# Fetching attention's first pair during the projection, and reordering stores and loads around that border

## The chip, the cores and the metric

The kernel runs on one core of a Trainium2 chip. Its time is the device time of one execution, in microseconds; of several runs the median is given.

## The reference, cut to what matters

Four blocks follow one another on x (4 batches of 1024 tokens, 256 wide), each with a residual: a state-space layer, a mixture of 8 experts, causal attention with 16 heads of 16, and a mixture of 16 experts. The change lies in the third.

```python
x = x + _L0_attn_ref(_layernorm(x, axis=-1), ...)      # state-space layer
x = x + _L0_ffn_ref(_layernorm(x, axis=-1), ...)       # mixture of experts
x = x + _L1_attn_ref(_layernorm(x, axis=-1), L1_attn_W_qkv, L1_attn_W_o)
x = x + _L1_ffn_ref(_layernorm(x, axis=-1), ...)       # mixture of experts

# _L1_attn_ref
qkv = jnp.einsum('bsi,oi->bso', x, W_qkv)
Q, K, V = jnp.split(qkv, 3, axis=-1)
Q, K, V = (to_heads(Q), to_heads(K), to_heads(V))
Q, K = (apply_rope(Q), apply_rope(K))
scores = jnp.einsum('bhqd,bhkd->bhqk', Q, K) / jnp.sqrt(jnp.float32(d_k))
scores = jnp.where(causal, scores, -jnp.inf)
attn = jax.nn.softmax(scores, axis=-1)
out = jnp.einsum('bhqk,bhkd->bhqd', attn, V)
```

## The kernel before, in words

The program is a row of phases, each an `nc.Block()` in which the five engines run their own instruction lists in order and meet at its end. Two of them matter here, with a short block between that clears semaphores (L2413).

`project_qkv` (L1231) works through the 4096 tokens in 8 groups of 512. A tick handles several groups at once, each at another step:

- GpSimd gathers the two expert outputs of each token (L1339, 8 gathers a group, half of them ahead of `rsqrt` and half behind), and later adds the turned halves (`add_turned`, L1353 and L1355).
- DVE adds the experts to x (L1383, L1387), takes the statistics, multiplies by the rotation's tables (`rotate`, L1416), adds the last sum (L1407) and makes the low part of queries and keys (`rest`, L1421): qk minus its rounded high part.
- ScalarE normalises (L1453), copies the values out of PSUM (`copy_v`, L1467), copies the transposed tokens (L1460) and rounds queries and keys to the high part (`round_qk`, L1476).
- TensorE transposes and projects (L1503, L1514, L1521).
- SP (the sync engine) issues all direct DMAs, in this order in tick t: `store_x2(t)` (L1295), `load(t+2)` of x (L1291), `store_v(t-1)` (L1299, 512 KB), `store_qk(t-3)` (L1311 for the high, L1313 for the low parts, 8 DMAs of 256 KB, each with a wait for ScalarE's or DVE's part). At the end it waits for all stores. `round_qk(g)` waits for the stores of group g-2, whose buffers it fills.

ScalarE's order in tick t is `normalise(t)`, `copy_v(t-1)`, `copy_xn(t)`, `round_qk(t-2)`; the ticks run to 9. TensorE has nothing after group 7's values in tick 7.

`attention` (L1537) works through 32 pairs of heads (8 per batch). Queries and keys of a pair lie in one of four buffers (`qs`, `ks`); 8 DMAs of 128 KB bring them (`load(p)`, L1656, issue at L1649), each 32 rows of 4 KB to 16 partitions. All of them land in partitions 0 to 63; row 96 of `qs` gets the negated row maxima. TensorE's list is written out by step, 18 steps a pair. In a step it does, for pair q, one chunk of scores with keys in the rows (`chunk`, L1841), and for a pair one and a half ahead one or two pieces of scores with queries in the rows (`piece`, L1827), whose maxima DVE takes (L1766). After a pair's pieces the maxima are transposed (L1833), negated by ScalarE (L1778) and written by SP into the pair's buffer (`row`, L1671); `chunk(p, 0)` waits for that row. ScalarE takes the exponentials (L1785), GpSimd masks them (L1738) after it has laid out the values (L1730), and TensorE multiplies them with the values (L1857). Until pair 0 has its row, TensorE fills the steps with matmuls that compute nothing (`keep_busy`, L1864), 7 of them ahead of the first piece. `piece(p, 0)` waits for the pair's 8 loads.

SP's order is: `load(0)` (4 DMAs of queries; the 4 of keys are issued by ScalarE at L1795), `load(1)`, then in tick 1 `row(0)`, `load(2)`, `load_v(0)` (L1664, 1 MB of values); in tick t from 2 on `load(t+1)`, now and then `load_v`, `store(t-4)`, `row(t-1)`. `load(p)` for p of 4 or more waits for the last chunk of pair p-4. At step 72 ScalarE issues a fetch of expert weights (4 MB in two DMAs, L2491).

Of the kernel before, what the change touches and what calls it, by code (L numbers as in the profile page):

```python
# [4 lines left out]
FP32 = mybir.dt.float32  # L5
# [1224 lines left out]

def project_qkv(nc, sb, pb, sem, c, x_dram, outputs, kept, sum_dram, w_qkv_dram, rope_dram, qkt_dram, v_dram):  # L1231

# [50 lines left out]
    def live(g):  # L1283
        return 0 <= g < groups

    with nc.Block() as block:
        @block.sync
        def _(sp):
# [30 lines left out]
            for tick in range(groups + 3):  # L1319
                if live(tick):  # L1320
                    store_x2(tick)
                if live(tick + 2):
                    load(tick + 2)
                if live(tick - 1):
                    store_v(tick - 1)
                if live(tick - 3):
                    store_qk(tick - 3)
            for s in range(2):
# [111 lines left out]
        def _(act):  # L1440
# [36 lines left out]

            for tick in range(groups + 2):
                if live(tick):
                    normalise(tick)  # L1480
                if live(tick - 1):
                    copy_v(tick - 1)
                if live(tick):
                    copy_xn(tick)
                if live(tick - 2):
                    for n in range(NB):
                        round_qk(tick - 2, n)

        @block.tensor
# [46 lines left out]

def attention(nc, sb, pb, sem, c, qkt_dram, v_dram, heads_dram, inv_dram, fetch):  # L1537

# [13 lines left out]
    RT, RS = 3, 4  # L1552
    ks = sb("t_ks", [P, 2 * RINGQ, SEQ], FP32R)
    qs = sb("t_qs", [P, 2 * RINGQ, SEQ], FP32R)
    v_raw = sb("t_v_raw", [P, NC, DM])
# [62 lines left out]
    filled, set_up = sem("t_filled"), sem("t_set_up")  # L1618
    qk_loaded = [sem(f"t_qk_loaded{s}") for s in range(RINGQ)]
    row_loaded = [sem(f"t_row_loaded{s}") for s in range(RINGQ)]  # L1620
# [22 lines left out]
    def live(p):  # L1643
        return 0 <= p < pairs

    def load_rows(eng, p, dst, which, part, hl):
        s = p % RINGQ
        rows = hl * 2 * DM + which * DM + (p % PAIRS) * 2 * HD
        eng.dma_start(dst[part * HD:(part + 1) * HD, 2 * s:2 * s + 2, :].bitcast(FP32),  # L1649
                      qkt_dram[rows:rows + 2 * HD, bass.ts(p // PAIRS, SEQ)].rearrange("(h d) t -> d h t", h=2)).then_inc(qk_loaded[s], 16)  # L1650

    with nc.Block() as block:
        @block.sync
        def _(sp):
            def load(p):
                wait(sp, st_done, NX * (p - RINGQ) + NX)  # L1656
                for part in range(4):
                    load_rows(sp, p, qs, 0, part, part % 2)
                    if p > 0:
                        load_rows(sp, p, ks, 1, part, part // 2)  # L1660

# [4 lines left out]
            def row(p):  # L1666
                s = p % RINGQ
                if p < RINGQ:
                    sp.wait_ge(rows_filled, 2 * p + 1)
                sp.wait_ge(neg_ready, p + 1)  # L1670
                sp.dma_start(qs[MAX_ROW:MAX_ROW + 1, 2 * s:2 * s + 2, :].bitcast(FP32).rearrange("o h (c q) -> o (h c) q", c=NC),  # L1671
                             neg_max[:, p % 2, :].bitcast(FP32)).then_inc(row_loaded[s], 16)
# [4 lines left out]

            load(0)
            load(1)
            for tick in range(1, pairs + 5):  # L1680
                if tick > 1 and live(tick + 1):
                    load(tick + 1)
                if tick % PAIRS == PAIRS // 2 and live(tick + PAIRS // 2):
                    load_v(tick // PAIRS + 1)
                if live(tick - 4):
                    store(tick - 4)
                if live(tick - 1):
                    row(tick - 1)
                if tick == 1:
                    load(2)  # L1690
                    load_v(0)
                if tick == pairs:
                    for s in range(2):
                        sp.wait_ge(stored[s], 8 * PAIRS * (BATCH - 1))
                    sp.wait_ge(vs_ready, BATCH)
                    for b in range(BATCH - 1):
                        sp.dma_start(sums[:, b, :], sums_of_batch(heads_dram, b)).then_inc(sums_loaded, 16)
                if tick == pairs + 1:
                    sp.wait_ge(inv_ready, 1)
                    for b in range(BATCH - 1):  # L1700
                        sp.dma_start(inverse_of_batch(inv_dram, b), sums[:, b, :]).then_inc(inv_stored, 16)
# [5 lines left out]
        def _(pool):  # L1707
            def zero_rows(p):
                nc.gpsimd.memset(qs[KS:P, 2 * p:2 * p + 2].bitcast(FP32), 0.0).then_inc(rows_filled, 1)

# [8 lines left out]
            for p in range(1, RINGQ):  # L1719
                zero_rows(p)  # L1720
                nc.gpsimd.memset(ks[KS:P, 2 * p:2 * p + 2].bitcast(FP32), 1.0).then_inc(rows_filled, 1)
            pool.wait_ge(rows_filled, 2 * RINGQ - 1)
# [27 lines left out]
        def _(dve):  # L1750
            nc.vector.memset(row_max[:], 0.0).then_inc(filled, 1)
            nc.vector.memset(ks[KS:P, 0:2].bitcast(FP32), 1.0).then_inc(filled, 1)
            nc.vector.memset(ps_o[:], 0.0).then_inc(filled, 1)
# [19 lines left out]
        def _(act):  # L1773
# [19 lines left out]

            for part in range(4):
                load_rows(act, 0, ks, 1, part, part // 2)  # L1795
            for step in range(LAST):
# [12 lines left out]
        def _(pe):  # L1809
# [9 lines left out]
            def piece(p, x):  # L1819
                head, qc, k0, keys = row_pieces[p % 2][x]  # L1820
                at = 2 * (p % RINGQ) + head
                if x == 0:
                    pe.wait_ge(qk_loaded[p % RINGQ], 128 * (p // RINGQ + 1))
                    if p < RINGQ:
                        pe.wait_ge(rows_filled, 2 * p + 1)
                bank_free(p, x)
                nc.tensor.matmul(bank_of(p, x)[:, 0:keys], qs[0:MAX_ROW, at, qc * P:(qc + 1) * P], ks[0:MAX_ROW, at, k0:k0 + keys],  # L1827
                                 start=True, stop=True).then_inc(s_done, 1)
# [6 lines left out]
            def chunk(p, i):  # L1835
                at = 2 * (p % RINGQ) + i // NST
                if i == 0:
                    pe.wait_ge(row_loaded[p % RINGQ], 16 * (p // RINGQ + 1))
                wait(pe, exp_ready, NX * p + i - RT + 1)
                for kc, q0, col, width in chunks[i % NST]:  # L1840
                    last = nc.tensor.matmul(ps_st[(NX * p + i) % RT][:, col:col + width], ks[:, at, kc * P:(kc + 1) * P], qs[:, at, q0:q0 + width],  # L1841
                                            start=True, stop=True)
# [509 lines left out]
def build(nc, x, w_in, w_abc, w_out, norm_w, gate_w, gate_b, w1, b1, w2, b2, w_qkv, w_o, rope, w_route, w_gu, w_d,  # L2352
# [36 lines left out]
    with ExitStack() as whole:  # L2389
        keep = lambda n, s, d=FP32: whole.enter_context(nc.sbuf_tensor(n, s, d))  # L2390
        sem = lambda n: whole.enter_context(nc.semaphore(n))
        moe0_loaded, moe1_loaded = sem("moe0_loaded"), sem("moe1_loaded")

        x_in = flat(x)
        with ExitStack() as first:
# [13 lines left out]


            phase(project_qkv, c, x1_dram, outputs[0], kept, x2_dram, w_qkv, rope, qkt_dram, v_dram)

# [6 lines left out]
        wgu_sb = wsb("wgu_sb", [P, KD, E1 * 2 * F1])  # L2419
        phase(attention, c, qkt_dram, v_dram, headst_dram, inv_dram, lambda eng: load_moe1_up(eng, moe1_loaded, wgu_sb, w_gu))  # L2420
        wd_sb = wsb("wd_sb", [P, F1 // P, E1 * DM])
# [116 lines left out]
```

## Time and profile before

| | us |
|---|---|
| median of 3 runs | 1808.42 |
| lowest, highest | 1807.4, 1811.73 |
| the profiled execution | 1807.72 |
| its span, from the first to the last instruction | 1805.7 |

The profile is of one execution. Times in its rows count from the start of the span. PE is TensorE's matmuls, PEld its weight loads, DVE VectorE, ACT ScalarE, POOL GpSimd, SP the sync engine; a q behind a name is the engine's instruction queue, which issues DMAs. PEclk is the granted clock of TensorE: 1.00 is 2.4 GHz and 0.50 is 1.2 GHz. The projection lies at 750 to 914 us, attention at 915 to about 1427.

### The profile page before, as it was taken

To read this page: it belongs to the slowest core of one execution; us is meant where nothing else is said; L and a number is where in the kernel's file an instruction comes from. 1 tells how busy PE (TensorE), PEld (TensorE's weight loads), DVE (VectorE), ACT (ScalarE), POOL (GpSimd) and SP (SyncE) were. 2 spreads that over 40 slices of the span, in tenths; PEclk is the share of its full clock that TensorE was granted. 3 is DMA by queue.
4 is the path that set the end of the run, shared out by engine and by line. 5 is a ranking of instruction groups with operands and counts; after the bars stand their busy time and mean duration, and the time that the engine had idled before them with its cause. 6 is when DMAs were issued, how large, how long until landed. Compare 5 with 4: busy or idle time off the path is not lost. (4 is left out here: it accounts for less than half of the span.)

```text
span 1805.7 us, 29737 instructions
## 1 busy us (share of the span) xinstructions
PE 1558.0 (86%) x9335; PEld 1100.6 (61%) x9335; DVE 1000.2 (55%) x3322; ACT 721.5 (40%) x1519; POOL 563.2 (31%) x991
## 2 busy tenths in 40 slices
PE   1999999982999999688668899999999667399998
PEld 0577777771666666444345566666666356288787
DVE  1245444442222222268847788888888267365566
ACT  0444444430222222134305676777777422144410
POOL 2122333344000000278532322333222238500076
PEclk9899999995999999898878999999999877599999
DMA  8100111112222221359767867667664276445444
GB/s 297 55 24 25 47 48 48 36 52 93 73 65 65 65 65 59 102 177 298 230 134 107 190 94 116 90 93 116 94 90 66 74 224 223 168 147 158 135 138 142
DMA packets 150807, 204.08 MB, mean 113 GB/s; under 512 B 20352, under 2 KB 119168, under 8 KB 150400
## 3 DMA queue, kind: packets, MB, share of 16 engines
q1 hardware_dynamic: 102496, 129.53, 32.0%
q10 hardware_dynamic: 35872, 39.09, 6.4%
q0 software_dynamic: 12288, 33.57, 5.9%
q8 instruction: 80, 1.31, 0.3%
q14 instruction: 71, 0.58, 0.1%
HBM read 116.91 MB, written 84.93 MB: 112 GB/s over the span
## 5 line engine op out<-in xcount | busy, mean ns | idle before, releaser
L1785 ACT ACTIVATE t_probs<-t_ps_st 128x512 f32<-128x512 f32 x576 | 313.4, 596 | 145.0 <-PE t_ps_st L1841 135.3
L1766 DVE CUSTOM_DVE_ANT_0 t_seen<-t_ps_s,t_later 128x512 bf16<-128x512 f32 (+3 forms) x512 | 286.1, 587 | 34.9 <-PE t_ps_s L1827 32.5
L1827 PE MATMUL t_ps_s<-t_ks,t_qs 96*128 96x512 f32 (+3 forms) x768 | 252.6, 369 | 5.9 <-DMA t_ks<-qkt_dram 5.7
L1841 PE MATMUL t_ps_st<-t_qs,t_ks 128*128 128x512 f32 (+3 forms) x768 | 245.8, 369 | 12.0 <-DMA t_qs<-t_neg_max 6.4
L1738 POOL TENSOR_SCALAR_AFFINE_SELECT t_probs<-t_probs 128x128 f32<-128x128 f32 x512 | 137.3, 302 | 319.3 <-ACT t_probs L1785 317.5
L1841 PEld LDWEIGHTS t_ps_st<-t_qs,t_ks 128*128 128x128 f32 x768 | 138.8, 192 | 87.2 <-ACT t_probs L1785 42.3
L1766 DVE CUSTOM_DVE_ANT_0 t_seen<-t_ps_s,t_later,t_first_max 128x512 bf16<-128x512 f32 (+3 forms) x256 | 140.6, 549 | 54.8 <-PE t_ps_s L1827 54.8
L1339 POOL DMA_INDIRECT d_ye<-outputs_dram,r_pos_all x64 | 64.6, 1009 | 327.5 <-POOLq L1099 309.7
L1857 PE MATMUL t_ps_o<-t_probs,t_vs 128*17 128x256 f32 (+1 forms) x2560 | 156.6, 364 | 0.5 <-issue 0.5
L1827 PEld LDWEIGHTS t_ps_s<-t_ks,t_qs 96*128 96x128 f32 x768 | 141.9, 194 | 24.3 <-DMA t_ks<-qkt_dram 6.5
L832 PE MATMUL ps_h<-w_in,xnt 128*128 128x512 f32 x256 | 125.5, 615 | 22.4 <-ACT xnt L666 22.4
L1131 PE MATMUL m_ps_h<-w_sb,m_xt 128*128 x284 | 135.6, 600 | 0.0
L1146 PE MATMUL m_ps_y<-w_sb,m_ht 128*128 x568 | 134.2, 379 | 0.0
L1202 ACT ACTIVATE m_xt<-m_ps_x 128x256 f32<-128x256 f32 x150 | 57.6, 384 | 174.8 <-PE m_ps_x L1124 174.6
L1174 DVE TENSOR_TENSOR m_h<-m_ps_h,b_sb 128x512 f32<-128x512 f32 x71 | 49.1, 692 | 131.6 <-PE m_ps_h L1131 129.7
L2268 POOL DMA_INDIRECT f_ye<-outputs_dram,r_pos_all x64 | 63.1, 986 | 170.8 <-POOLq L1099 151.6
L1212 ACT ACTIVATE m_ht<-m_ps_ht 128x128 f32<-128x128 f32 (+1 forms) x150 | 63.9, 426 | 128.0 <-PE m_ps_ht L1139 128.0
L1146 PEld LDWEIGHTS m_ps_y<-w_sb,m_ht 128*128 128x128 f32 x568 | 102.5, 190 | 11.0
L1857 PEld LDWEIGHTS t_ps_o<-t_probs,t_vs 128*17 128x17 f32 x2560 | 59.3, 97 | 72.9 <-issue 28.8
L1124 PE MATMUL m_ps_x<-ident,m_x_t 128*128 128x128 f32 x300 | 58.9, 279 | 41.4 <-DMA m_x_t<-gathered_dram 40.3
L351 POOL TENSOR_TENSOR xi<-xi,sig_z 128x512 f32<-128x512 f32 x32 | 40.6, 1269 | 160.3 <-ACT sig_z L678 160.2
L1185 DVE TENSOR_TENSOR m_y<-m_ps_y,b_sb 128x256 f32<-128x256 f32 x71 | 30.2, 425 | 104.7 <-PE m_ps_y L1146 104.7
(309 smaller groups left out, 2782.0 us busy)
## 6 DMA issues: line engine op xcount, KB each, us to landing
m_x_t<-gathered_dram SPq DMA_DIRECT2D x150, 128.0 KB, 2.0
outputs_dram<-m_y ACTq DMA_DIRECT2D x150, 128.0 KB, 1.7
t_qs<-qkt_dram SPq DMA_DIRECT2D x128, 128.0 KB, 5.8
t_ks<-qkt_dram SPq DMA_DIRECT2D x124, 128.0 KB, 6.1
qkt_dram<-d_hi SPq DMA_DIRECT2D x32, 256.0 KB, 4.0
qkt_dram<-d_lo SPq DMA_DIRECT2D x32, 256.0 KB, 4.0
headst_dram<-t_att SPq DMA_DIRECT2D x32, 256.0 KB, 7.1
x_t<-in_x_dram SPq DMA_DIRECT2D x8, 512.0 KB, 4.4
```

The costliest lines, as they stand in the source:

```text
L832: last = nc.tensor.matmul(ps_h[h][:], xnt[:, n % 2, j, :], w_in[:, j, h * DI:(h + 1) * DI], start=(j == 0), stop=(j == KD - 1))
L1131: last = nc.tensor.matmul(ps_h[t % 2][:], xt[:, t % 2, j, :], w_up[:, j, bass.ts(expert[t], width)], start=(j == 0), stop=(j == KD - 1))
L1146: last = nc.tensor.matmul(ps_y[t % 2][:], ht[:, t % 2, j, :], w_down[:, j, bass.ts(expert[t], DM)], start=(j == 0), stop=(j == blocks - 1))
L1212: nc.scalar.activation(ht[:, t % 2], ps_ht[t % 2][:], ACT.Relu if relu else ACT.Copy).then_inc(ht_ready, 1)
L1339: nc.gpsimd.indirect_dma_start(out=ye[:, g % 2, j, i, :], out_offset=None, in_=outputs[:, :], in_offset=bass.IndirectOffsetOnAxis(ap=kept[ ...
L1738: nc.gpsimd.affine_select(out=diag, in_=diag, compare_op=ALU.is_ge, fill=0.0, base=0, pattern=[[1, P]], channel_multiplier=-1).then_inc(ma ...
L1766: nc.vector.tensor_tensor_reduce(out=seen[:, (NP * p + x) % (RS + 1), 0:keys], in0=bank_of(p, x)[:, 0:keys], in1=masks, scale=1.0, scalar= ...
L1785: nc.scalar.activation(probs[:, p % 2, i // NST, base:base + STC], ps_st[(NX * p + i) % RT][:], ACT.Exp, scale=HD ** -0.5).then_inc(exp_re ...
L1827: nc.tensor.matmul(bank_of(p, x)[:, 0:keys], qs[0:MAX_ROW, at, qc * P:(qc + 1) * P], ks[0:MAX_ROW, at, k0:k0 + keys], start=True, stop=Tru ...
L1841: last = nc.tensor.matmul(ps_st[(NX * p + i) % RT][:, col:col + width], ks[:, at, kc * P:(kc + 1) * P], qs[:, at, q0:q0 + width], start=Tr ...
L1857: last = nc.tensor.matmul(ps_o[32 * g:32 * g + VR, col:col + width], vs[:, (p // PAIRS) % 2, kc, 2 * (p % PAIRS) + head, :], probs[:, p % ...
L2268: nc.gpsimd.indirect_dma_start(out=ye[:, g % R, j, i, :], out_offset=None, in_=outputs[:, :], in_offset=bass.IndirectOffsetOnAxis(ap=kept[ ...
```

## The change

- `project_qkv` gets a function `fetch`. ScalarE calls it at tick 8, after two waits for the stores of groups 0 and 1: it issues the 8 loads of pair 0.
- Pair 0's buffers (`q_first`, `k_first`) and semaphore are therefore made before the projection and handed to both phases; `qs` and `ks` become lists of four buffers each. ScalarE's four loads at the start of attention and SP's `load(0)` go.
- In the projection SP issues `store_qk(t-3)` ahead of `store_v(t-1)`.
- In tick 8 ScalarE does `copy_v(7)` after `round_qk(6)` instead of before it.
- In attention SP issues `load(2)` in tick 1 ahead of `row(0)`; behind `row(0)` comes `load_v(0)` alone, and then `load(3)`.

```diff
-def project_qkv(nc, sb, pb, sem, c, x_dram, outputs, kept, sum_dram, w_qkv_dram, rope_dram, qkt_dram, v_dram):
+def project_qkv(nc, sb, pb, sem, c, x_dram, outputs, kept, sum_dram, w_qkv_dram, rope_dram, qkt_dram, v_dram, fetch):
...
                     load(tick + 2)
+                if live(tick - 3):
+                    store_qk(tick - 3)
                 if live(tick - 1):
                     store_v(tick - 1)
-                if live(tick - 3):
-                    store_qk(tick - 3)
...
             for tick in range(groups + 2):
+                if tick == groups:
+                    for s in range(2):
+                        act.wait_ge(qk_stored[s], 32 * NB)
+                    fetch(act)
                 if live(tick):
                     normalise(tick)
-                if live(tick - 1):
+                if live(tick) and live(tick - 1):
                     copy_v(tick - 1)
                 if live(tick):
                     copy_xn(tick)
                 if live(tick - 2):
                     for n in range(NB):
                         round_qk(tick - 2, n)
+                if tick == groups:
+                    copy_v(tick - 1)
...
+def load_head_rows(eng, p, dst, which, part, hl, qkt_dram, loaded):
+    rows = hl * 2 * DM + which * DM + (p % PAIRS) * 2 * HD
+    eng.dma_start(dst[part * HD:(part + 1) * HD].bitcast(FP32),
+                  qkt_dram[rows:rows + 2 * HD, bass.ts(p // PAIRS, SEQ)].rearrange("(h d) t -> d h t", h=2)).then_inc(loaded, 16)
+
+
+def load_heads(eng, p, q, k, qkt_dram, loaded):
+    for part in range(4):
+        load_head_rows(eng, p, q, 0, part, part % 2, qkt_dram, loaded)
+        load_head_rows(eng, p, k, 1, part, part // 2, qkt_dram, loaded)
...
-    ks = sb("t_ks", [P, 2 * RINGQ, SEQ], FP32R)
-    qs = sb("t_qs", [P, 2 * RINGQ, SEQ], FP32R)
+    ks = [k_first] + [sb(f"t_ks{i}", [P, 2, SEQ], FP32R) for i in range(1, RINGQ)]
+    qs = [q_first] + [sb(f"t_qs{i}", [P, 2, SEQ], FP32R) for i in range(1, RINGQ)]
...
-    qk_loaded = [sem(f"t_qk_loaded{s}") for s in range(RINGQ)]
+    qk_loaded = [first_loaded] + [sem(f"t_qk_loaded{s}") for s in range(1, RINGQ)]
...
             def load(p):
                 wait(sp, st_done, NX * (p - RINGQ) + NX)
-                for part in range(4):
-                    load_rows(sp, p, qs, 0, part, part % 2)
-                    if p > 0:
-                        load_rows(sp, p, ks, 1, part, part // 2)
+                load_heads(sp, p, qs[p % RINGQ], ks[p % RINGQ], qkt_dram, qk_loaded[p % RINGQ])
...
-            load(0)
             load(1)
             for tick in range(1, pairs + 5):
-                if tick > 1 and live(tick + 1):
+                if live(tick + 1):
                     load(tick + 1)
...
                 if tick == 1:
-                    load(2)
                     load_v(0)
...
-            for part in range(4):
-                load_rows(act, 0, ks, 1, part, part // 2)
...
+            q_first, k_first = (ahead.enter_context(nc.sbuf_tensor(n, [P, 2, SEQ], FP32R, side="right")) for n in ("t_qs0", "t_ks0"))
+            phase(project_qkv, c, x1_dram, outputs[0], kept, x2_dram, w_qkv, rope, qkt_dram, v_dram,
+                  lambda eng: load_heads(eng, 0, q_first, k_first, qkt_dram, first_loaded))
```

The rest of the diff hands the buffers through and puts `qs[s]` for `qs[:, 2 * s:...]`.

## Rows read from the trace of the kernel before

**Rows 1.** The page, busy time of each engine with its share of the span.

```profile
PE 1558.0 (86%) x9335; PEld 1100.6 (61%) x9335; DVE 1000.2 (55%) x3322; ACT 721.5 (40%) x1519; POOL 563.2 (31%) x991
```

**Rows 2.** The timeline 860 to 935: start, duration, engine, line, what, [idle before].

```profile
891.43 0.36 SPq L1299 DMA_DIRECT2D v_dram<-d_v  x1
...
902.08 2.50 DVE L1421 TENSOR_TENSOR d_lo<-d_qk,d_hi 128x512 f32<-128x512 f32 x4 [4.89 <-ACT d_hi L1476]
...
909.99 0.70 SPq L1313 DMA_DIRECT2D qkt_dram<-d_lo  x1
```

**Rows 3.** Windows: length, busy (instructions) of each engine, PEclk, DMA share, GB/s.

```profile
870.00:878.00 8.00, 3.77 (x17) 2.57 (x16) 7.97 (x17) 2.33 (x5) 6.25 (x4) 0.98 0.33 111
878.90:912.90 34.00, 11.67 (x34) 6.35 (x32) 19.57 (x26) 8.39 (x16) 9.79 (x6) 0.70 0.85 277
...
895.00:910.00 15.00, 0.00 (x0) 0.00 (x0) 4.58 (x6) 2.19 (x4) 3.31 (x2) 0.50 1.01 332
```

**Rows 4.** The timeline 914 to 969: attention's first issues and TensorE's waits for DMAs.

```profile
914.97 1.79 ACTq L1649 DMA_DIRECT2D t_ks<-qkt_dram  x4
...
915.01 7.63 PE L1864 MATMUL t_ps_st<-causal,ident 128*128 128x512 f32 x14 [24.23 <-PEq L2413]
...
926.45 0.79 PE L1827 MATMUL t_ps_s<-t_ks,t_qs 96*128 96x512 f32 x1 [3.82 <-DMA t_ks<-qkt_dram]
...
927.41 0.69 DVE L1766 CUSTOM_DVE_ANT_0 t_seen<-t_ps_s,t_later 128x512 bf16<-128x512 f32 x1 [9.44 <-PE t_ps_s L1827]
...
955.21 0.50 PE L1827 MATMUL t_ps_s<-t_ks,t_qs 96*128 96x512 f32 x1 [1.88 <-DMA t_ks<-qkt_dram]
...
968.02 0.80 PE L1841 MATMUL t_ps_st<-t_qs,t_ks 128*128 128x512 f32 x1 [4.83 <-DMA t_qs<-t_neg_max]
```

**Rows 5.** Windows of attention's start: PE, PEld, DVE, ACT, POOL, PEclk, DMA share, GB/s.

```profile
920.00:925.00 5.00, 2.64 (x8) 1.04 (x6) 0.00 (x0) 0.00 (x0) 5.00 (x4) 1.00 1.07 127
926.40:932.20 5.80, 5.75 (x15) 4.74 (x16) 2.80 (x10) 0.00 (x0) 5.74 (x3) 0.50 1.01 120
927.40:935.00 7.60, 7.60 (x28) 6.35 (x26) 5.37 (x19) 0.00 (x0) 4.83 (x2) 0.68 0.67 79
935.00:942.00 7.00, 7.00 (x36) 6.14 (x35) 6.94 (x29) 0.00 (x0) 0.00 (x0) 1.00 0.00 0
956.00:973.00 17.00, 11.98 (x45) 8.00 (x44) 7.96 (x29) 6.20 (x12) 7.09 (x25) 0.61 1.08 144
```

**Rows 6.** The timeline of SP's queue: the rows of maxima of pairs 0, 1, 2, 4, 5.

```profile
943.47 0.59 SPq L1671 DMA_DIRECT2D t_qs<-t_neg_max  x1
...
958.70 0.54 SPq L1671 DMA_DIRECT2D t_qs<-t_neg_max  x1
...
981.36 0.51 SPq L1671 DMA_DIRECT2D t_qs<-t_neg_max  x1
...
1017.55 0.52 SPq L1671 DMA_DIRECT2D t_qs<-t_neg_max  x1
...
1032.05 0.52 SPq L1671 DMA_DIRECT2D t_qs<-t_neg_max  x1
```

**Rows 7.** The timeline at 865, DVE's first addition of group 7.

```profile
865.67 1.98 DVE L1383 SCALAR_TENSOR_TENSOR d_part<-d_ye,r_prob_all,d_x 128x256 f32<-128x256 f32 x4 [1.81 <-issue]
```

**Rows 8.** The timeline 880 to 892: low parts of group 5, group 7's values, group 6's low parts.

```profile
880.94 3.56 DVE L1421 TENSOR_TENSOR d_lo<-d_qk,d_hi 128x512 f32<-128x512 f32 x4
...
889.08 0.60 ACT L1467 ACTIVATE d_v<-d_ps_v 128x512 f32<-128x512 f32 x1 [7.25 <-PE d_ps_v L1521]
...
891.96 3.56 DVE L1421 TENSOR_TENSOR d_lo<-d_qk,d_hi 128x512 f32<-128x512 f32 x4 [1.00 <-ACT d_hi L1476]
```

**Rows 9.** The timeline at 944, the first of pair 2's loads on SP's queue.

```profile
944.11 0.58 SPq L1649 DMA_DIRECT2D t_qs<-qkt_dram  x1
```

**Rows 10.** The rows of maxima (L1671), all 32, from issue to landing.

```profile
DMA to landing us min/median/max: 1.8/1.8/9.3
```

**Rows 11.** The timeline at 992, ScalarE's second issue of expert weights.

```profile
992.03 6.77 ACTq L2491 DMA_DIRECT2D wgu_sb<-in_w_gu_dram  x1
```

## What the change should do to the time, worked out before its run

> **What bounds the kernel now.** I read first the page's totals: TensorE is busy for 86% of the span [rows 1], and only where it stands still, or runs slowly, is there much to be had. The change touches the end of the projection and the start of attention, so every cost is read from that stretch, 860 to 1032 us. The views are the order of time of SP's queue, windows with the DMA share and the granted clock, and the rows in which TensorE sat idle for a DMA.
>
> The projection ends on transfers. DVE's last low part is done by 904.6 and still the next block starts only at 914.97, because SP issues 24 stores of 256 KB back to back behind v_dram's store at 891.43, the last at 909.99 [rows 2, 4]. From 895 to 910 the DMA engines are full: share 1.01 at 332 GB/s. From 870 to 878 the share is 0.33 [rows 3]. So the bound there is the DMA engines' work, and SP's 0.79 us per issue follows it.
>
> Attention starts on transfers too. TensorE waits 3.82 us for pair 0, 1.88 us for pair 2 and 4.83 us for pair 1's row of maxima [rows 4]. After each wait its clock falls to the lower level: granted 0.50 in 926.4 to 932.2 and 0.61 in all of 956 to 973, against 1.00 at 935 to 942 [rows 5]. What this costs is read in the spacing of the rows of maxima, one per pair: 15.23 and 22.66 us at the start, 36.19 for the next two together, and 14.50 from there on [rows 6].
>
> **The change, part by part.** (1) The projection's stores. SP issues store_qk(t-3) ahead of store_v(t-1). In ticks 3 to 6 the same bytes flow, some us earlier in each tick. A tick's 2.1 MB of stores (6.3 us at 332 GB/s) then lie behind x2's store and x's load, and are still there when the tick's last gather is issued, so the gather meets other traffic as before. DVE's whole wait ahead of add_experts is 1.81 us in such a tick [rows 7]. I take 0 and keep -1 and +3.6 (half of that wait in four ticks) as bounds.
>
> At the end it counts. Group 4's stores move from 879 on to 870 to 877, where the DMA engines have room. Group 5's move from 891.8 to 880.3 and on: their low parts come from 881.6 to 884.5 [rows 8]. Behind v's store at 891.4 there are 16 stores instead of 24. If SP's issue were the bound, the end would come 8 x 0.79 = 6.3 us earlier.
>
> (2) The fetch of pair 0 by ScalarE: eight loads of 128 KB at its tick 8. The waits ahead of them are for groups 0 and 1, stored long before. ScalarE stood idle there for 7.25 us, up to 889.08, until TensorE had the last values [rows 8]. At 0.45 us each (four took 1.79 [rows 4]) the issues end near 885.5. Queued behind them are round_qk(6) and then copy_v(7). The rounding fits into what is left of the gap, and copy_v(7) can't start before 889.08, so no value is delayed; DVE, which waited 1.00 us for that rounding [rows 8], no longer does. The fetch isn't free on the DMA engines, though: such loads move at 127 GB/s with the share at 1.07 [rows 5]. 1.05 MB is 8.3 us of full DMA.
>
> Sum by DMA work: from 878.9 (v's store) to 912.9 it is 0.85 x 34 = 28.9 us [rows 3]. Group 4 leaves (6.3) and the fetch comes (8.3): 30.9. No gap is left but about 1 us around 880.5, as the low parts arrive one by one. The end is 878.9 + 30.9 + 1 = 910.8 instead of 912.9, some **2.0 us** saved. The bounds are 6.3 (issue alone) and -1 (the tail takes the fetch whole against group 5's stores, 8.3 against 6.3, and gives back 1 us by the earlier low parts).
>
> One rule of the Trainium skill prices the fetch otherwise. DMA: Bandwidth & Descriptors, Specifications, has pieces of 512 B or more run at line rate and gives about 358 GB/s for HBM to one core. By that the fetch, in rows of 4 KB, would be an estimated 2.9 us, and the saving would be the 6.3 of the issues. This case's row, 127 GB/s at share 1.07 [rows 5], disagrees, and the measurement decides.
>
> (3) Attention's start. Pair 0 is there, so after its 14 warming matmuls (915.01 to 922.64) TensorE goes straight on: **3.8 us**. DVE's fills and the mask were done by 918, since DVE stood idle for 9.44 us ahead of its first piece [rows 4]. TensorE stays at the higher clock too. In 927.4 to 935 DVE is busy for 5.37 of 7.6 us, and for 6.94 of 7 once the clock is up [rows 5]. So DVE is the next bound and **2.2 us** go; by the clock alone it would be 2.9 (5.8 us at half). Nothing at all, if another gap cools TensorE, is the lower end.
>
> (4) Pair 2's loads now follow pair 1's at once. Both together are 17 us of DMA, so pair 2 lands some 19 us after the block's start; before, it was wanted 38.4 us in (953.33) [rows 4], and by the new count some 32. Pair 1 lands 10 us in and is wanted 21 us in. The 1.88 us go, but DVE had a backlog and its own work per pair stays, so of the 15.23 I count **1.4 us**, with 0.7 (what leaves 14.5) and 1.9 as bounds.
>
> (5) Behind row(0) SP now has only the values and pair 3. Before, pair 2 lay ahead of them (from 944.11 [rows 9]), so row(1), issued at 958.70 on the same queue, landed 9.3 us later, where the median is 1.8 [rows 6, 10]. Now values (1.05 MB at the stores' rate, 3.2 us) and pair 3 (8.3 to 9 us) end 13 to 14 us behind row(0); row(1) is issued 13.8 to 14.5 behind it and lands by 17, and chunk(1,0) wants it 4.5 us after its issue (963.19 against 958.70), so about 18.5. The wait of 4.83 goes, and with it the lower clock of 956 to 973. The interval 22.66 becomes 14.5: **8.2 us**. The lower end is 4.8, the wait alone.
>
> What is late next: ScalarE's own fetch of expert weights, whose second issue holds it for 6.77 us [rows 11]. It is tied to step 72 and stays, and so do the 36.19 us. All behind attention moves as one block.
>
> Sum: 2.0 + 3.8 + 2.2 + 1.4 + 8.2 = 17.6 us. The profiled execution took 1807.72 us (span 1805.7), 0.7 under the median of 1808.42. 1807.72 - 17.6 = 1790.1, and by the median **1790.8 us**.
>
> **The rivals.** A: the waits go, but TensorE stays at the lower clock in part of the start. Then 2.0 + 3.8 + 0 + 0.7 + 4.8 = 11.3 us go: 1797. For it speaks the 0.61 over 17 us after a wait of only 1.88 [rows 4, 5]; against it, that the clock is 1.00 from 935 to 942 with the same work. Chance 0.13.
>
> B: row(1) is still caught behind pair 3, since its margin is some 1.5 us and the time of a pair's loads is known to 10%. If it lands 3 us late the clock falls again: 2.0 + 3.8 + 2.2 + 1.4 + 2 = 11.4, again 1797. Chance 0.12.
>
> C: the stores are bound by issue, and the gathers gain: 6.3 + 3.6 in place of 2.0, in sum 25.5: 1783. Against it speaks share 1.01 [rows 3]. Chance 0.12.
>
> D, slower: ScalarE is held by its own DMA issues. Place: tick 8, ahead of round_qk(6) and copy_v(7). If each of the eight took 6.77 us, as the second weight fetch does [rows 11], ScalarE would be free at 936 instead of 885.5. v's store and 16 stores (14.2 us of DMA) would follow, so the stage would end some 39 us later, less the 15.6 us of attention: 1832. It decides for slower once the eight together take over 24 us, 3 us each. Against it: the four issues at 914.97 beside SP's took 1.79 us in all [rows 4]. Chance 0.03.
>
> E: the fetch takes DMA time from the tail, and attention only swaps the later waits for others of DVE and ScalarE: -1 + 3.8 in sum, 1805.6. Chance 0.04.
>
> **How the numbers follow.** Forecast (12 to 22 us saved): 0.56. With A, B and most of C, the range 1783 to 1799 holds about 8 in 10. About 0.3%, 5.4 us, is what a measurement can tell from no change here. Faster by more: 0.56 + 0.13 + 0.12 + 0.12, of which I keep 0.92. Within 0.3%: 0.05. Slower: 0.03.
>
> **What would show it.** In the changed kernel's profile the block behind the projection starts about 2 us earlier, with the DMA share near 1 from 881 to the end. TensorE's first piece follows the warming matmuls without a gap, at a granted clock of 1.00. The first row of maxima is issued 22.5 us after the block's start instead of 28.5, and the next ones 13.8 and 14.5 apart. No wait of TensorE for pair 2 or for row(1) is left. It would be wrong if the clock falls anyway, if row(1) still lands over 5 us after its issue, or if ScalarE's eight issues take over 8 us.

## The result

| | us |
|---|---|
| before, median | 1808.42 |
| after, median of 5 runs | 1789.04 (1786.89 to 1790.61) |
| after over before | 0.9888, 95% interval 0.9875 to 0.9901 |
| the profiled execution of after, and its span | 1787.32, 1785.6 |

The forecast was 1790.8, 17.6 us less; 19.4 came. The changed kernel run again beside other kernels gave 1788.47 against 1809.03, ratio 0.9888. In the two traces 20.1 us of the span are gone, and by the sixth row of maxima 20.4 (1011.65 instead of 1032.05), so what lies behind that row took back only 0.3.

SP's queue in the changed kernel, from x2's last store to the rows of maxima of pairs 0 to 2 and 5. The first load at 912.60 is attention's start:

```profile
872.11 0.36 SPq L1295 DMA_DIRECT2D x_dram<-d_x  x1
...
894.84 0.37 SPq L1299 DMA_DIRECT2D v_dram<-d_v  x1
...
907.38 0.69 SPq L1313 DMA_DIRECT2D qkt_dram<-d_lo  x1
912.60 0.34 SPq L1545 DMA_DIRECT2D t_qs<-qkt_dram  x1
...
933.97 0.59 SPq L1680 DMA_DIRECT2D t_qs<-t_neg_max  x1
...
947.34 0.54 SPq L1680 DMA_DIRECT2D t_qs<-t_neg_max  x1
960.87 0.51 SPq L1680 DMA_DIRECT2D t_qs<-t_neg_max  x1
...
1011.65 0.51 SPq L1680 DMA_DIRECT2D t_qs<-t_neg_max  x1
```

Set against [rows 2, 4, 6], the stretches are these (x2(3) and x2(7) are the stores of x2 in ticks 3 and 7, at 808.26 and 869.26 before, 808.36 and 872.11 after):

| stretch | before | after | measured | forecast |
|---|---|---|---|---|
| x2(3) to x2(7), four ticks | 61.00 | 63.75 | +2.75 | 0 |
| x2(7) to attention's start | 45.71 | 40.49 | -5.22 | -2.0 |
| attention's start to row(0) | 28.50 | 21.37 | -7.13 | -6.0 |
| row(0) to row(1) | 15.23 | 13.37 | -1.86 | -1.4 |
| row(1) to row(2) | 22.66 | 13.53 | -9.13 | -8.2 |
| row(2) to row(5) | 50.69 | 50.78 | +0.1 | 0 |

Attention's start looks as forecast. The timeline of TensorE shows the 14 warming matmuls, and the first piece right behind them with no wait in brackets, where [rows 4] had 3.82:

```profile
912.64 7.39 PE L1869 MATMUL t_ps_st<-causal,ident 128*128 128x512 f32 x14 [18.45 <-PEq L2420]
...
919.68 0.58 PE L1832 MATMUL t_ps_s<-t_ks,t_qs 96*128 96x512 f32 x1
```

And the windows of the changed kernel (PE, PEld, DVE, ACT, POOL, PEclk, DMA share, GB/s): a full clock (1.00) and DVE busy all the time in 925 to 932. The first row is the end of the projection, to be held against the 0.85 and 277 of [rows 3]:

```profile
881.50:910.30 28.80, 11.99 (x32) 6.59 (x32) 20.72 (x26) 9.12 (x17) 9.80 (x6) 0.74 0.97 294
...
925.00:932.00 7.00, 7.00 (x37) 6.15 (x35) 7.00 (x29) 0.00 (x0) 4.87 (x2) 1.00 0.80 90
```

### The profile page after: what moved, and what is told of

It is laid out like the page before. It is cut to its first block and busy times, and to the rows that moved or that the text cites. A ratio compares the mean times of both kernels' runs of the same rounds, so it can differ in the third digit from the quotient of the medians.

```text
span 1785.6 us, 29738 instructions
## 1 busy us (share of the span) xinstructions
PE 1557.8 (87%) x9335; PEld 1100.2 (62%) x9335; DVE 999.4 (56%) x3322; ACT 721.7 (40%) x1519; POOL 564.4 (32%) x991
## 5 line engine op out<-in xcount | busy, mean ns | idle before, releaser
L1832 PE MATMUL t_ps_s<-t_ks,t_qs 96*128 96x512 f32 (+3 forms) x768 | 248.7, 364 | 0.5 <-ACT t_neg_max L1785 0.5
L1773 DVE CUSTOM_DVE_ANT_0 t_seen<-t_ps_s,t_later,t_first_max 128x512 bf16<-128x512 f32 (+3 forms) x256 | 140.6, 549 | 50.8 <-PE t_ps_s L1832 50.8
L1832 PEld LDWEIGHTS t_ps_s<-t_ks,t_qs 96*128 96x128 f32 x768 | 139.5, 191 | 18.1 <-DVE t_first_max L1773 1.6
```

Of the source, the lines that this page charges most:

```text
L1773: nc.vector.tensor_tensor_reduce(out=seen[:, (NP * p + x) % (RS + 1), 0:keys], in0=bank_of(p, x)[:, 0:keys], in1=masks, scale=1.0, scalar= ...
L1832: nc.tensor.matmul(bank_of(p, x)[:, 0:keys], q[0:MAX_ROW, head, qc * P:(qc + 1) * P], k[0:MAX_ROW, head, k0:k0 + keys], start=True, stop=T ...
```

## The experiments

The experiments ran on three chips, each beside the kernel before. On the first of them (e1 to e4) all kernels were slower, the kernel before at 1831.72 us, so times are compared by their ratios, and stretches within the projection and attention by the traces. How well unchanged code repeats differs by stretch. The ticks in the old order repeat within 0.3 us (60.69 to 61.00), in the new order only within 3 (62.04 to 65.02). The first row comes 27.15 to 28.50 us after attention's start without the fetch (e5 apart, whose edit moves it) and 21.19 to 22.75 with it. The kernel before and e8 have the same attention, and their next two intervals are 15.23 and 22.66 against 16.25 and 21.36.

The end repeats least: the old code took 45.71 us in the kernel before, 45.48 in e7 and 48.74 in e5. TensorE's clock makes that difference: the projection of group 7's queries and keys (16 matmuls) took 7.11 us in e7, 7.99 in the kernel before and 10.16 in e5, with a granted clock of 1.00, 0.70 and 0.50 over its first 3 us, and v's last store follows it. The timelines of TensorE in e7 and then e5:

```profile
877.46 7.11 PE L1514 MATMUL d_ps_qk<-d_xnt,d_w_qk 128*128 128x512 f32 x16 [0.77 <-DVE d_by L1416]
```

```profile
877.81 10.16 PE L1514 MATMUL d_ps_qk<-d_xnt,d_w_qk 128*128 128x512 f32 x16 [0.77 <-DVE d_by L1416]
```

The end can be taken apart at v's last store. In every kernel but e1 that store is issued 14.2 us plus the time of these 16 matmuls after x2(7) (7.11 to 10.17 us; 8.54 in the changed kernel). From it to attention's start it is 23.54, 24.18 and 24.39 us in the kernel before, e7 and e5, which have 24 stores behind it, 23.91 in e1, and 17.66 to 18.16 in all kernels with 16 stores behind it. This second part repeats within 1 us, and it is the better measure of what an edit does.

In the table "ticks" is x2(3) to x2(7), "end" is x2(7) to attention's start, "rows" are the first row's distance from that start and the next two intervals.

| kernel | ratio (95%) | ticks | end | rows |
|---|---|---|---|---|
| before | 1 | 61.00 | 45.71 | 28.50, 15.23, 22.66 |
| changed | 0.9888 (0.9875 to 0.9901) | 63.75 | 40.49 | 21.37, 13.37, 13.53 |
| changed again (c1) | 0.9888 (0.9867 to 0.9909) | 63.99 | 40.71 | 21.31, 13.38, 13.53 |
| e1 old store order | 0.9927 (0.9904 to 0.9949) | 60.75 | 50.31 | 21.19, 13.38, 13.53 |
| e2 new order from tick 7 | 0.9870 (0.9851 to 0.9889) | 60.73 | 41.93 | 21.68, 13.39, 13.75 |
| e3 no fetch ahead | 0.9920 (0.9891 to 0.9948) | 62.04 | 41.53 | 28.37, 13.39, 13.53 |
| e4 pair 2 behind row(0) | 0.9944 (0.9924 to 0.9964) | 63.89 | 41.94 | 22.11, 15.30, 22.93 |
| e5 before, warm gap | 0.9994 (0.9979 to 1.0008) | 60.69 | 48.74 | 25.70, 15.25, 22.98 |
| e6 values copied first | 0.9890 (0.9847 to 0.9934) | 65.02 | 40.21 | 22.75, 13.38, 13.54 |
| e7 before, pair 2 early | 0.9922 (0.9903 to 0.9941) | 60.75 | 45.48 | 27.15, 13.39, 13.52 |
| e8 before, new order alone | 0.9990 (0.9978 to 1.0002) | 63.99 | 42.02 | 27.49, 16.25, 21.36 |
| e9 new order from tick 6 | 0.9879 (0.9857 to 0.9901) | 61.57 | 41.71 | 21.70, 13.38, 13.53 |
| e10 e9, weights in two steps | 0.9869 (0.9845 to 0.9894) | 61.90 | 41.80 | 21.68, 13.39, 13.52 |

**The store order, undone in the changed kernel (e1).**

```diff
-                if live(tick - 3):
-                    store_qk(tick - 3)
                 if live(tick - 1):
                     store_v(tick - 1)
+                if live(tick - 3):
+                    store_qk(tick - 3)
```

> The changed kernel with one part undone: SP stores values ahead of queries and keys in every tick, as before the change. Theory 1 (read from the two traces): the new order has two effects of opposite sign. In ticks 3 to 6 the stores of queries and keys lie ahead of the gathers in the DMA engines, and the four ticks from x2(3) to x2(7) take 63.75 us instead of 61.0; at the end it saves. So with the old order the four ticks take 61.0 again, the end takes the 45.7 us of before from x2(7) to attention's start, with the fetch in the gap ahead of the last values at no cost, and attention starts at about 915.0: 2.4 us later than in the changed kernel, 1791.4. Theory 0 (the prediction's): the ticks don't change, the fetch is 8.3 us of exclusive DMA time and finds only 5 us of gap: attention starts at 918, 1794.4.

The ticks came back to 60.75, as theory 1 has it. But the end took 50.31 us, longer than in the kernel before and than both theories gave. The cause stands in ScalarE's and SP's rows of e1:

```profile
892.90 2.19 ACT L1476 ACTIVATE d_hi<-d_qk 128x512 fp32r<-128x512 f32 x4 [10.64 <-DMA qkt_dram<-d_lo]
...
895.00 1.06 ACT L1467 ACTIVATE d_v<-d_ps_v 128x512 f32<-128x512 f32 x2
...
896.09 0.37 SPq L1299 DMA_DIRECT2D v_dram<-d_v  x1
```

round_qk(6) waits for group 4's stores, which in the old order are issued together with the fetch and land late. ScalarE stands for 10.64 us, copy_v(7) waits behind it, and v's store goes out 26.4 us after x2(7) instead of 22.2 in the kernel before (869.26 to 891.43), with 24 stores behind it. So the fetch and the reordered last tick need the new store order at the end. The end is 9.8 us longer than in the changed kernel. 6.2 us of that lie behind v's store (23.91 instead of 17.76), about what the order is worth by itself. The store itself comes 18.3 us behind x2(7), the 16 matmuls not counted, instead of 14.2: these 4.1 us are the price of the fetch and the reordered tick under the old order (the matmuls, 8.15 us, gave 0.4 back). Which of the two makes them was not tried. The eight issues of the fetch took 7.8 us here (879.83 to 887.59), close to the 8 us that the prediction named as a sign against it.

**The store order, new only at the end (e2, e9).** e2 has it from tick 7, e9 from tick 6:

```diff
-                if live(tick - 3):
-                    store_qk(tick - 3)
-                if live(tick - 1):
+                if tick < groups - 1 and live(tick - 1):
                     store_v(tick - 1)
+                if live(tick - 3):
+                    store_qk(tick - 3)
+                if tick >= groups - 1 and live(tick - 1):
+                    store_v(tick - 1)
```

> The changed kernel with the new store order only from tick 7 on, the old one in ticks 3 to 6. Theory 1: the four ticks take 61.0 us again and the end keeps its 40.5 us from x2(7) to attention's start, so attention starts 2.8 us earlier than in the changed kernel, near 909.8, and the time is 1786.2. Theory 0: the order in ticks 3 to 6 costs nothing, the time is that of the changed kernel, 1789.0.

> The changed kernel with the new store order only from tick 6 on (e2 had it from tick 7 on), where no load of x lies between x2's store and the stores of queries and keys. Theory 1: only ticks with three things queued ahead of the gathers (x2's store, x's load, the stores of queries and keys) lose by the new order, so the four ticks take 61.0 us, and with group 3's stores out of the way of group 4's the end takes the 40.5 us of the changed kernel instead of e2's 41.9. Attention starts 2.8 us earlier than in the changed kernel: ratio to the kernel before 0.9875. Rival: tick 6 loses 1 us as the others do and the clock in tick 8 decides the rest: as e2, 1.3 us before the changed kernel.

The ticks fell to 60.73 and 61.57, so the cost of the new order in the earlier ticks is real. Tick 6 of e9, which has the new order but no load of x, took 15.26 us, as it did with the old one. In e10, whose projection has the same code, tick 6 took 15.79. The end kept most of its gain but was 1.0 to 1.4 us longer than the changed kernel's, so the 40.5 us that theory 1 gave both times were missed. v's store came 23.8 and 23.7 us after x2(7) instead of 22.7, because the 16 matmuls ahead of it took 9.59 and 9.47 us instead of 8.54; TensorE's clock in e9 was 0.50 to 0.62 from 876 to 882. From v's store on it was 18.2 and 18.1 us, against 17.8. Whether the edit or chance gave the lower clock is open. By their traces both start attention earlier than the changed kernel, by 1.35 us (e2, 911.25) and, beside c1 on one chip, by 0.8 us (e9, 910.41 against 911.22). The ratios (0.9870 and 0.9879 against 0.9888) point the same way, with overlapping intervals.

**The store order alone, in the kernel before (e8).** The edit of e1 the other way round.

> The kernel before with the new store order of the projection alone, without fetch or any change in attention. Theory 1: the four ticks take 62 to 64 us instead of 61.0, x2(7) to attention's start 41.5 instead of 45.7 (as without the fetch in e3), so attention starts 1.6 us earlier and the time is 1.6 us less, ratio 0.999. Theory 0: ticks as before and 8 issues of 0.79 us saved, 6.3 us less, ratio 0.9965.

Ticks 63.99, end 42.02: +3.0 and -3.7 us. From v's store to attention's start it is 17.66 us instead of 23.54, the changed kernel's gain in full and without a fetch; the rest of the difference in the end is the 16 matmuls, 10.17 us here. Ratio 0.9990, as theory 1 gave it: alone, the reorder is worth nothing that these runs can tell.

**Why the ticks lose.** The second half of group 4's gathers (tick 3), the kernel before and then the changed one, each with its time from issue to landing:

```profile
L1339 POOL DMA_INDIRECT d_ye<-outputs_dram,r_pos_all x4: 953/978/1057, 811.7 to 815.6; - x4
DMA to landing us min/median/max: 2.7/3.5/4.2
```

```profile
L1339 POOL DMA_INDIRECT d_ye<-outputs_dram,r_pos_all x4: 952/978/1055, 811.8 to 815.7; - x4
DMA to landing us min/median/max: 5.7/5.9/6.1
```

And DVE's addition that waits for them, before and after:

```profile
819.91 1.91 DVE L1383 SCALAR_TENSOR_TENSOR d_part<-d_ye,r_prob_all,d_x 128x256 f32<-128x256 f32 x4 [1.90 <-issue]
```

```profile
821.54 1.67 DVE L1383 SCALAR_TENSOR_TENSOR d_part<-d_ye,r_prob_all,d_x 128x256 f32<-128x256 f32 x4 [3.41 <-issue]
```

The gathers are issued at the same time and land 2.4 us later at the median. In the old order the last of them is issued before the first of the tick's stores of queries and keys (816.01), in the new one these stores go out from 809.32 on. DVE then waits 1.5 us longer; that it is the gathers it waits for is read from the code, since the rows name no releaser. Tick 3 grew by 1.3 us. In the next two ticks the median rose from 4.4 to 5.2 and from 4.1 to 5.2 us, and they grew by 0.4 and 1.0. That the order costs the ticks is shown (e1, e2, e8); that the gathers are how it does is what the traces suggest, and was not tried by itself. The size is uncertain: with this order e3's ticks took 62.04 us and e6's 65.02.

**No fetch ahead (e3).** Pair 0 is loaded at attention's start, the rest is as changed.

```diff
             for tick in range(groups + 2):
-                if tick == groups:
-                    for s in range(2):
-                        act.wait_ge(qk_stored[s], 32 * NB)
-                    fetch(act)
...
+            for part in range(4):
+                load_head_rows(sp, 0, qs[0], 0, part, part % 2, qkt_dram, first_loaded)
             load(1)
...
+            for part in range(4):
+                load_head_rows(act, 0, ks[0], 1, part, part // 2, qkt_dram, first_loaded)
```

> The changed kernel without the fetch in the projection: pair 0 is loaded at attention's start as before (queries by SP, keys by ScalarE), all other parts kept. Theory 1: the fetch was hidden, since it and the stores ran beside each other (294 GB/s over 28.8 us), and attention starts within 0.7 us of the changed kernel's 912.6. Theory 0: the fetch costs the tail at least 2 us, so attention starts at 910.6 or earlier. Both: TensorE waits 3.8 us for pair 0 again and runs its first pieces at the lower clock, so that the first row of maxima comes 28.5 us after attention's start instead of 21.4. In sum 7.1 us more by theory 1, 1796; 5 us by theory 0, 1794.

The end took 41.53 us without the fetch and 40.49 and 40.71 with it, and from v's store on 18.08 against 17.76 and 17.91: with the new order the fetch costs the projection nothing. From 890 to 893.8 the DMA share of e3 is 0.00; the changed kernel's is 1.03 from 892 to 894.8. So the fetch fills a gap ahead of v's store. Attention started at 911.88, within 0.7 us of 912.60, and the first row came 28.37 us after it. So the fetch ahead is worth 7.0 us, all of it in attention; the times say 5.8 (0.9920 against 0.9888), with wide intervals. Why it is cheap shows in the changed kernel's DMA queues from 881 to 893 (packets, MB, share of 16 engines), the fetch being all of q10:

```profile
q1 hardware_dynamic: 1301, 1.93, 57.7%
q10 hardware_dynamic: 384, 1.05, 38.8%
```

38.8% of 12 us is 4.7 us of the DMA engines for the 1.05 MB, in which q1 stored beside it. In the kernel before, where such loads run only beside each other, from 920 to 925:

```profile
q1 hardware_dynamic: 128, 0.36, 61.0%
q10 hardware_dynamic: 103, 0.27, 45.6%
```

1.07 x 5 us for 0.63 MB, or 8.8 us for 1.05 MB. It isn't the second queue that slows them: in the changed kernel SP's queue alone moved 120 GB/s at share 1.05 with such loads (920 to 930). So the share over 1 was a limit of these loads among themselves, and left room for stores. Why it is so is open.

**Pair 2's place (e4, e7).** e4 takes it back in the changed kernel; e7 makes it alone in the kernel before.

```diff
-                if live(tick + 1):
+                if tick > 1 and live(tick + 1):
                     load(tick + 1)
...
                 if tick == 1:
+                    load(2)
                     load_v(0)
```

> The changed kernel with one part undone: pair 2's loads go behind the first row of maxima again, ahead of the values. The prediction's theory: TensorE waits for pair 2 again, then for row(1), which lands some 9 us after its issue, and loses its clock after each. The intervals of the rows go from 13.37 and 13.53 back to 15.2 and 22.7: 11.0 us more, 1800. Rival: only the waits themselves come back (1.9 + 4.8) and the clock costs nothing beside them: 6.7 us more, 1795.7.

> The kernel before with one part done alone: pair 2's loads right behind pair 1's, and only the values and pair 3 behind the first row of maxima. Theory: the wait for pair 0 stays (first row 28.5 us after attention's start), the waits for pair 2 and for row 1 go with their clock, and the intervals are 13.4 and 13.5 us instead of 15.2 and 22.7: 11 us less, ratio 0.994. Rival (pair 2 in the queue delays pair 0 or pair 1, whose loads run at that time): the first row comes later than 28.5 and part of the 11 us is lost.

e4's rows of maxima (pairs 0, 1, 2), then e7's of pairs 1 and 2:

```profile
941.94 0.59 SPq L1680 DMA_DIRECT2D t_qs<-t_neg_max  x1
957.24 0.54 SPq L1680 DMA_DIRECT2D t_qs<-t_neg_max  x1
980.17 0.51 SPq L1680 DMA_DIRECT2D t_qs<-t_neg_max  x1
```

```profile
953.40 0.54 SPq L1671 DMA_DIRECT2D t_qs<-t_neg_max  x1
966.92 0.51 SPq L1671 DMA_DIRECT2D t_qs<-t_neg_max  x1
```

15.30 and 22.93 in e4, 13.39 and 13.52 in e7: 11.3 us of intervals come back in e4 and 11.0 go in e7, and the pair's place alone makes them. TensorE's waits for DMAs in e4 are 2.0 and 4.8 us together, so the other 4.5 us are what comes with them, the lower clock among it. e7 gives 0.9922, about 14 us (11 to 17 by the interval), the largest single part; by the traces it is 11.4 from attention's start to the sixth row. Pair 2 in the queue took nothing from pair 0, whose wait was 3.2 us.

**The clock by itself (e5).** TensorE's wait for pair 0 is filled with matmuls in the kernel before:

```diff
-            for i in range(6):
+            for i in range(10):
                 keep_busy(i, 4 * P)
```

> The kernel before with four more warming matmuls at attention's start (10 instead of 6 blocks), which fill TensorE's 3.8 us wait for pair 0 and take nothing else away. Theory (the clock is a term of its own): the first pieces start as before, some 11.5 us after attention's start, but at the higher clock, and the first row of maxima comes 2.2 to 2.9 us earlier, at 25.6 to 26.3 us instead of 28.5. Rival (the pieces are bound by DVE or by the arriving pair anyway): 28.5 stays. The later waits for pair 2 and row 1 stay in both, so the time changes by less than 3 us.

The matmuls end when the pair is there, and the clock of 925 to 930 is 1.00 instead of 0.55; the row of maxima is counted from SP's first load:

```profile
916.47 2.20 SPq L1649 DMA_DIRECT2D t_qs<-qkt_dram  x5
...
942.17 0.59 SPq L1671 DMA_DIRECT2D t_qs<-t_neg_max  x1
```

```profile
927.89 0.59 PE L1827 MATMUL t_ps_s<-t_ks,t_qs 96*128 96x512 f32 x1
```

```profile
925.00:930.00 5.00, 5.00 (x20) 3.18 (x18) 1.19 (x5) 0.00 (x0) 5.00 (x3) 1.00 1.09 129
```

The first piece runs 11.4 us after attention's start, as before (11.5), and the row comes at 25.70 instead of 28.50. But the kernel before is not the only measure. From the first piece to the row it takes 17.0 us in the kernel before and in e3, and 15.8 in e7 and e8, which waited 3.2 and 3.4 us instead of 3.8 and 3.7: in the 5.8 us from that piece on the clock was 0.50 in the first two and 0.72 and 0.71 in the others. Without the wait (changed kernel, e4, e5, e6) it takes 14.3. So the clock's share is 1.5 or 2.7 us, by how soon it comes back, with the wait left as it was. The ratio, 0.9994, can't tell so little from nothing; the stretch can.

**ScalarE's last tick (e6).**

```diff
-                if live(tick) and live(tick - 1):
+                if live(tick - 1):
                     copy_v(tick - 1)
...
-                if tick == groups:
-                    copy_v(tick - 1)
```

> The changed kernel with one part undone: in its tick 8 ScalarE copies group 7's values ahead of rounding group 6, as before the change; the fetch stays ahead of both. The prediction's theory: DVE waits about 1 us for the rounding again, but the DMA engines are full by then, so the end moves by less: x2(7) to attention's start 40.5 to 41.2 us. Rival (the chain of rounding, low parts and stores sets the end): all of the 1.0 us or more comes back, 41.5 to 42.5.

DVE waits 1.10 us for the rounding again, and the end takes 40.21 us (17.94 from v's store on): the reorder of the last tick moves nothing that can be seen.

**What is left in attention (e10).**

```diff
                 if step == 4 * NX:
-                    fetch(act)
+                    fetch(act, 0)
+                if step == 5 * NX:
+                    fetch(act, 1)
```

> The kernel of e9 with one thing more: ScalarE issues the second half of the expert weights at step 90 instead of right behind the first at step 72. Theory (the prediction's: the intervals of 19.4 and 16.5 us that are left come from ScalarE's hold of 6.3 us at that second issue): the hold goes, and the two intervals fall to 14.5 to 15.5 each: about 6 us less than e9, ratio 0.9845. Rival: the first issue is held in its place, or the 4 MB themselves slow the loads of the pairs, and the two intervals stay at 33 us or more in sum.

ScalarE's second issue takes 0.40 us instead of e9's 6.54, so the hold is gone. But the intervals from row(2) on are 14.58, 17.67 and 16.41, in sum 48.66 against 50.68 in e9. The first one lost 5.0 us and the next two took 3.0 back, TensorE now waiting 3.2 us in two places for a row of maxima. So 2.0 us went instead of the 6 that were expected, and the sum of the first two intervals, 32.25, is short of the rival's 33 too. What holds those rows was not tried. e10 has the lowest ratio beside the kernel before, 0.9869; that it or e9 or e2 beats the changed kernel is likely by the traces and not shown by the times.

## Why the prediction was right, step by step

**(1) and (2), the projection: right in sum (2.37 against 2.0) by luck, wrong in both terms.** The step that failed first is "the gather meets other traffic as before", with 0 and a bound of -1 for four ticks; they cost 2.75 to 3.0 us in the changed kernel, c1, e8 and against e2, and 1.0 to 4.0 over all kernels. I had looked at what is queued when the last gather is issued, and took a backlog in either order for the same. But in the old order that backlog only begins with v's store, as the gathers land; in the new one it is already there when they are issued. Rival C had even given the gathers a gain.

The second is the end's sum, 2.0 for what measured 5.2. Its term for the fetch, 8.3 us "of full DMA", was mis-sized: 4.7 us, since loads and stores ran beside each other. The rate of such loads was read where nothing but such loads runs, and can't be carried over. With 4.7 in its place the sum would have given 5.7, near the 5.2. From v's store on the changed kernel needs 17.8 us to attention's start, as e3 does without any fetch (18.1), so what was still in flight at v's store did not move the end: eight stores fewer behind it gave 5.8 us (23.54 to 17.76), and 0.6 of it went to the slower 16 matmuls. Whether those 5.8 us are the time of 8 issues or of 2.1 MB in the DMA engines can't be told, since both come to 6.3. By the Trainium skill (DMA: Bandwidth & Descriptors, Specifications) the prediction had estimated the load at 2.9 us; the measured 4.7 lies between that and 8.3, and the 5.2 us are near the 6.3 that it led to.

ScalarE was held by its eight issues hardly longer than forecast: 881.69 to 885.94, 4.3 us against 3.6. Rival D's mechanism, ScalarE late ahead of copy_v(7), did appear in e1, mostly by the wait for group 4's stores, with issues of 7.8 us in all ahead of it. The step "the rounding fits into the gap" is true only because the store order moves group 4 ahead of the fetch; I had costed the two edits side by side. The 1.00 us of DVE's wait was gone and worth nothing (e6).

**(3), attention's start: right.** 7.13 us against 6.0: 4.4 up to the first piece, 3.8 of it the wait, and 2.7 behind it. e3 gives 7.0 for the fetch alone. For the clock, which the forecast had at 2.2 by DVE and at 2.9 by the clock alone, 1.5 was measured against e7 and e8 and 2.7 against the kernel before and e3: both figures lie in what the executions give, and the trace that the forecast read was one of the slower ones.

**(4) and (5), pair 2 and row(1): right in mechanism and size.** -1.86 and -9.13 against -1.4 and -8.2. e4 and e7 take them away and bring them alone. The steady 14.5 that I put for the interval of row(2) was too long: 13.5, as in the interval ahead of it. Rival A (a cold clock) and B (row(1) caught behind pair 3) fell: in the changed kernel rows of maxima land within 5.4 us everywhere, and the clock is 1.00 from 920 to 970. (It is 0.50 in 978 to 984, behind a wait of 4.26 us for ScalarE, which the kernel before has too, with 4.72.)

**"What is late next" was right in where and too simple in why.** Row(2) to row(5) stayed at 50.8. The hold of ScalarE is a cause of one of the three intervals, but with it gone (e10) only 2 of some 7 us over the steady 43.5 went.

## What to carry to other kernels

Moving a store ahead in a queue moves its traffic onto whatever else is then in flight: look at every transfer that lands in that stretch, first of all at those on the loop that sets the tick, and make the move only in the ticks where it pays. When TensorE waits at the start of a stage, count the wait and the slower pieces behind it as two terms; here one change of order in a queue removed 6.7 us of waits and 11.0 us of time. A prefetch is as cheap as the stretch it is put in, and its edits can depend on one another: here it costs nothing with the new store order and, together with the reordered last tick, 4.1 us with the old. And take a stretch apart before comparing it: split at one store, an end that varied by 3 us became a part that follows TensorE's clock and a part that repeats within 1 us.

## What the runs showed of the hardware that I had not expected

- Loads of 4 KB rows into 16 partitions each, alone on both queues, take 8.8 us for 1.05 MB with the DMA share at 1.07. Beside stores from all partitions the same loads took 4.7 us of the engines' time, and both queues together moved 248 GB/s (2.98 MB in 12 us). So in these traces a share over 1 didn't mean that the engines had no time for another kind of transfer.
- Four gathers issued while 2.1 MB of stores went out on another queue landed after 5.9 us at the median instead of 3.5.
- The same 16 matmuls of the projection took 7.11 to 10.16 us in three executions of the same code, and moved the end of the stage by 3 us. The granted clock over their first 3 us was 1.00 where they took 7.11 us, 0.70 where they took 7.99 and 0.50 where they took 10.16.
- A wait of TensorE of 3.2 to 3.8 us cost 1.5 or 2.7 us more behind it, by execution; filled with matmuls which compute nothing it was no shorter and this cost was gone.
